# Four row blocks of w2 per quantization step, and attention heads divided straight from PSUM

## The reference

```
x = x + attn_a(layernorm(x))        # RWKV-like time mix, 16 heads
x = x + ffn(layernorm(x))           # BitNet-like, 1024 -> 4096 -> 1024
x = x + attn_b(layernorm(x))        # linear attention, 16 heads, chunks of 128
x = x + ffn(layernorm(x))           # the same FFN and weights again
```

```
scale = 1.0 / clip(mean(abs(w)), 1e-5)
wq = clip(round(w * scale), -1, 1) / scale
```

```
out = (inter_num + intra_num) / (inter_den + intra_den + 1e-6)
```

## Time and profile before

| | us |
|---|---|
| median of 3 runs (7890.95 to 7900.04) | 7897.22 |
| profiled execution, its own time | 7890.33 |
| span of its slowest core (core 4) | 7889.3 |
| spans of the other cores | 7857.3 to 7881.8 |
| quantization of w1, both passes (32.9 to 380.95) | 348.1 |
| quantization of w2, both passes (380.95 to 877.16) | 496.2 |
| attention a to the end | the rest |

### The profile page before, as it was taken

The page is one execution under the profiler, slowest core; times in us unless marked ns, Lnnn a source line. Parts: engine busy times, 40 slices in busy tenths (PEclk is TensorE's granted clock), DMA queues, the critical chain, the costliest instruction groups (busy, mean ns, idle before and its releaser), DMA issues.

```text
span 7889.3 us, 43212 instructions; the slowest of 8 cores (7857.3 to 7889.3 us)
## 1 busy us (share of the span) xinstructions
PE 2812.7 (36%) x12246; PEld 1203.9 (15%) x12420; DVE 2521.9 (32%) x5263; ACT 1027.8 (13%) x1504; POOL 154.0 (2%) x276
## 2 busy tenths in 40 slices
PE   0000045554234334443423444444414334433333
PEld 0000022222111111111101222222201111111111
DVE  3423343232522332223214333333342332223221
ACT  0101111110200111101102111111110111101110
POOL 0000000000000000000000000000000000000000
PEclk9999976666566666665655656566656656666666
DMA  4222300001011101110130000000011101110012
GB/s 156 106 94 80 120 0 1 1 1 45 0 43 43 34 13 39 43 43 12 31 127 1 1 1 1 1 1 1 1 44 43 31 13 42 43 43 15 28 43 83
DMA packets 92856, 288.49 MB, mean 37 GB/s; under 512 B 13244, under 2 KB 13772, under 8 KB 87506
## 3 DMA queue, kind: packets, MB, share of 16 engines
q1 hardware_dynamic: 67798, 201.83, 7.6%
q0 software_dynamic: 24832, 83.90, 3.6%
HBM read 260.48 MB, written 25.17 MB: 36 GB/s over the span
## 4 chain that ended last, share of the span: by engine, by line
DVE 30%; PE 29%; DMA 16%; issue 11%; ACT 11%; DVEq 1%; SPq 1%; ACTq 0%; POOLq 0%
DMA wbuf<-w2q_hbm 9%; PE pb L849 7%; PE pb L968 5%; DMA sA<-w_t 5%; PE pb L483 3%; PE pb L1206 2%; DVE arenaB L924 2%; ACT sA L866 2%; PE pbf L931 2%; ACT sB L912 2%; DVE arenaB L466 1%; PE pb L656 1%; DVEq L105 1%; ACT arenaB L1083 1%; DVE arenaB L935 1%
## 5 line engine op out<-in xcount | busy, mean ns | idle before, releaser
L968 PE MATMUL pb<-wbuf,arenaB 128*128 128x512 bf16 x2000 | 773.2, 544 | 556.2 <-DMA wbuf<-w2q_hbm 523.2
L849 PE MATMUL pb<-warena,arenaB 128*128 128x512 bf16 x1986 | 584.2, 461 | 196.2 <-ACT sA L866 132.1
L931 PE MATMUL pbf<-ident,arenaB 128*128 128x128 bf16 x1024 | 129.5, 306 | 1259.8 <-DVE arenaB L924 1188.0
L990 DVE TENSOR_TENSOR res<-res,pb 128x512 f32<-128x512 f32 x64 | 39.7, 683 | 1345.4 <-PE pb L980 1345.4
L968 PEld LDWEIGHTS pb<-wbuf,arenaB 128*128 128x128 bf16 x2048 | 223.8, 121 | 1097.4 <-issue 1050.3
L873 DVE TENSOR_REDUCE fcol<-sA 128x1 f32<-128x2048 f32 x32 | 73.1, 2286 | 887.1 <-ACT sA L866 887.1
L849 PEld LDWEIGHTS pb<-warena,arenaB 128*128 128x128 bf16 x2048 | 229.8, 114 | 543.4 <-issue 398.6
L931 PEld LDWEIGHTS pbf<-ident,arenaB 128*128 128x128 bf16 x1024 | 99.0, 137 | 1297.5 <-issue 1297.5
L483 PE MATMUL pb<-warena,arenaB 128*128 128x512 bf16 x752 | 211.1, 448 | 160.8 <-DVE arenaB L466 160.0
L958 POOL DMA_DIRECT2D wbuf<-w2q_hbm x256 | 137.7, 538 | 6668.0 <-PE pb L968 6217.5
L836 PE MATMUL pbf<-ident,arenaB 128*128 128x128 bf16 x256 | 32.4, 307 | 612.9 <-DVE arenaB L830 612.9
(11 more groups left out here) (219 smaller groups left out, 4490.3 us busy)
## 6 DMA issues: line engine op xcount, KB each, us to landing
wbuf<-w2q_hbm POOLq DMA_DIRECT2D x256, 256.0 KB, 2.9
wbuf<-w2q_hbm SPq DMA_DIRECT2D x256, 256.0 KB, 2.8
sA<-w_t SPq DMA_DIRECT2D x16, 2048.0 KB
sA<-w_t SPq DMA_DIRECT2D x64, 512.0 KB
warena<-w1q_hbm SPq DMA_DIRECT2D x2, 8192.0 KB
res<-x SPq DMA_DIRECT2D x1, 8192.0 KB
w1q_hbm<-arenaB SPq DMA_DIRECT2D x8, 1024.0 KB, 4.8
w2q_hbm<-arenaB SPq DMA_DIRECT2D x32, 256.0 KB, 2.1
```

What stands on the lines that cost most here:

```text
L849: mms.append((lambda e, ic=ic, ot=ot, o0=o0: e.matmul(p["pb%d" % ot][:], g["xqT"][:, 128 * ic:128 * ic + 128], W[:, 4096 * ic + o0:4096 * ...
L931: self.emit("tensor", lambda e, r=r, i=i: e.transpose(p["pbf"][:, 128 * i:128 * i + 128], g["hqb"][:, 1024 * r + 128 * i:1024 * r + 128 * ...
L968: mms.append((lambda e, hc=hc, bk=bk, oh=oh, buf=buf, hqT=hqT: e.matmul(p[bk][:], hqT[:, 128 * hc:128 * hc + 128], buf[:, 512 * oh:512 * o ...
```

## The change

There are two edits.

First, `wquant_one` takes a `batch` argument: one chunk becomes `batch` blocks of 128 rows, seen as `[128, batch, ncols]`. For w1 nothing changes (batch 1, 8 chunks). For w2 the call goes from 32 chunks of 128 x 1024 to 8 chunks of 128 x 4 x 1024, so each load brings 2 MB, each sum runs over 4096 columns, the rounding runs on two pieces of 2048 columns instead of four of 1024, and each store writes 1 MB.

Second, `attn_b_head_post` no longer copies `nd` to SBUF. The add of 1e-6 and the multiply read PSUM. The marks `ndf` and `ndb`, which let TensorE write into the bank again, move from the copy to the multiply, three operations later.

```
-    def wquant_one(self, dram_in, dram_out, ncols, nch, iswcol):
+    def wquant_one(self, dram_in, dram_out, ncols, nch, iswcol, batch=1):
...
-        src = self.dram[dram_in].rearrange("(a p) o -> p a o", p=128)
-        dst = self.dram[dram_out].rearrange("(a p) o -> p a o", p=128)
-        stage = g["sA"][:, 0:ncols]
-        nh = (ncols + 2047) // 2048
+        src = self.dram[dram_in].rearrange("(a q p) o -> p a q o", p=128, q=batch)
+        dst = self.dram[dram_out].rearrange("(a q p) o -> p a q o", p=128, q=batch)
+        ncols_eff = ncols * batch
+        stage = g["sA"][:, 0:ncols_eff]
+        st3 = stage.rearrange("p (q o) -> p q o", o=ncols)
+        nh = (ncols_eff + 2047) // 2048
         for a in range(nch):
-            self.emit("sync", lambda e, a=a: e.dma_start(out=stage, in_=src[:, a, :]),
+            self.emit("sync", lambda e, a=a, st3=st3: e.dma_start(out=st3, in_=src[:, a]),
                       wait=(("ve", self.now("ve")),), inc="dW", n=16)
...
-                w = min(2048, ncols - 2048 * hh)
+                w = min(2048, ncols_eff - 2048 * hh)
...
-            self.emit("sync", lambda e, a=a: e.dma_start(out=dst[:, a, :], in_=g["wq_bf"][:, 0:ncols]),
-                      wait=(("ve", self.now("ve")),), inc="dWs", n=16)
+            self.emit("sync", lambda e, a=a: e.dma_start(
+                out=dst[:, a], in_=g["wq_bf"][:, 0:ncols_eff].rearrange(
+                    "p (q o) -> p q o", o=ncols)),
+                wait=(("ve", self.now("ve")),), inc="dWs", n=16)
...
-        self.wquant_one("w2_t", "w2q_hbm", C, 32, g["fcol"][:, 41:42])
+        self.wquant_one("w2_t", "w2q_hbm", C, 8, g["fcol"][:, 41:42], batch=4)
...
         dc, rc = 42 + (h % 2), 44 + (h % 2)
-        nsl = g["sB"][:, 1024 + 128 * (h % 2):1024 + 128 * (h % 2) + 65]
-        self.emit("vector", lambda e, nd=nd, nsl=nsl: e.tensor_copy(out=nsl, in_=nd),
-                  wait=(ndtn,), inc="ve")
+        self.emit("vector", lambda e, nd=nd, dc=dc: e.tensor_scalar_add(
+            out=g["fcol"][:, dc:dc + 1], in0=nd[:, 64:65], scalar1=1e-6), wait=(ndtn,), inc="ve")
+        self.vchain([
+            lambda e, dc=dc, rc=rc: e.reciprocal(out=g["fcol"][:, rc:rc + 1],
+                                                 in_=g["fcol"][:, dc:dc + 1]),
+            lambda e, h=h, nd=nd, rc=rc: e.tensor_scalar_mul(
+                out=g["ob_b"][:, 64 * h:64 * h + 64], in0=nd[:, 0:64],
+                scalar1=g["fcol"][:, rc:rc + 1]),
+        ], wait0=(("ve", self.now("ve")),))
         self.hz["ndf%d" % (h % 8)] = ("ve", self.now("ve"))
         self.hz["ndb%d" % (h % 2)] = ("ve", self.now("ve"))
-        self.vchain([
...
```

More of the change, by code:

```diff
@@ L699, in wquant_one @@
         self.set_free("pb6", "sc")
-        nel = float(nch * 128 * ncols)
+        nel = float(nch * 128 * ncols_eff)
         self.vchain([
```

## The result

The changed kernel takes 7656.67 us (median of 8 runs, 7649.04 to 7672.79) against 7895.98 us (8 runs): a ratio of 0.9698, 95% interval 0.9687 to 0.9709, 239 us less. The prediction was 7679 us, within 7650 to 7727. Its sign and mechanism hold; it is 22 us too high. The saving of 239 us lies just beyond the 238 us that its bounds add up to, and inside the range only by the margin that it left for the measurement.

What follows compares the result with a forecast made beforehand. No engine was taken as the bound; an edit is worth what it takes out of a serial loop. Quantization 141 plus attention b 77 is 218 us off 7890.3, giving 7672, or 7679 with the median's 6.9; range 7650 to 7727.

Steps and rivals of the forecast that it cites:

- What bounds the kernel: Whole kernel: chain spread over all engines, none the bound; an edit is worth what it takes out of a serial loop.
- Pass 1: First pass of w2's quantization: 8 turns of 13.2 us, saving 61 us, bounds 55 to 66.
- step from 512 KB to 1 MB: w2's pass 1 loads: 3.99 to 5.54 us, so 1.55 us per 512 KB more, 8.6 us for 2 MB.
- Pass 2: Second pass of w2's quantization: 245 us against 325.5, saving 80 us, bounds 68 to 88.
- The price of short runs beside the store: w2's pass 2: 0.6 us more per load for 4 KB rows, 0.4 us for the store in 2 KB rows.
- Heads: Attention b: 0.30 us net saved per head over 256 heads in series, 77 us, bounds 51 to 84.
- The three terms: Each head of attention b: copy-to-add step of 0.33 us gone, add from PSUM no dearer, multiply 0.03 us more.
- The added wait: Attention b: line 1120's matmul now waits for the multiply; the pair takes until 0.82 us, line 1150 starts at 0.96.
- cover: Attention b: slack before the two delayed matmuls hold up line 1150, shrinking from about 1 us to 0.14 us.
- Dear PSUM reads: Attention b rival: PSUM reads dear or PE late, head gains 0.20 us or less; 7712 us at 0.17; 10%.
- Loads that are no better per byte: w2 quantization rival: a 2 MB load takes four times a small one, 16 us; 7795 us; 4%.
- The clock: PE stretches rival: less idle beforehand and denser heads lower the granted clock; at 0.54 some 7990 us; 2%.

Runs made afterwards that it cites:

- e12: Changed kernel with w2's chunks dealt so each partition takes four neighbouring rows, 16 KB per run on load; 7637.97 us, ratio 0.9698.
- e5: Kernel before, copy kept, with the marks `ndf` and `ndb` moved behind the multiply; 7880.96 us, ratio 0.9999.
- e6: Changed kernel with the mark moved further, behind the next head's mask; 7655.19 us, ratio 0.9715.
- e7: Changed kernel with the mark moved behind the next head's cast; 7710.98 us, ratio 0.9783.
- e8: Changed kernel with mask and cast fused into one operation that writes bf16 straight from PSUM; 7584.41 us, ratio 0.9625.
- e2: Kernel before with only the second edit: no copy, add and multiply read PSUM; 7800.92 us, ratio 0.9892.
- the prefetch version: Changed kernel with both quantizations rebuilt: 1 MB pieces, two staging and two store tiles, loads issued ahead; 7434.44 us, ratio 0.9439.

## Why the prediction was right

**What bounds the kernel.** Right. Both edits took what their serial loops held and nothing came back elsewhere: no untouched stage moved by more than 3 us but the first, which lost 5.7 us with code that did not change. The other runs with the same code for w1 gave 371 to 376 us, so that is spread between executions. It may be some 6 of the 22 us by which the forecast was high; passes 1 and 2 of w2 are 12 more.

**Pass 1.** The structure (turn = load + 4.6 us) was right to 0.1 us. The mis-sized term is the load, 8.6 us forecast and 7.6 measured, which is 8 us on the changed side. Its step from 512 KB to 1 MB was read from single loads that happened to be long. The 1 MB load of 5.54 us was issued behind two small DMAs, but this is not the reason: the same load behind the same two DMAs took 4.95 us on core 2 of the same trace (first row), and 5.0 us in the median over the eight cores of all fourteen profiles (4.7 to 7.0). A 1 MB load with no DMA ahead of it took 4.88 us on core 4 (second row) and 5.0 in the median:

```profile
894.69 4.95 DMA sC<-wk_t
...
4064.94 4.88 DMA sC<-wq_t
```

The lower end of the forecast load, w1's 7.94 us, was no fixed point either: with the same code w1's loads were shorter in the changed kernel's execution (7.5 us in the median over the cores, 8.1 in the kernel before; 7.5 to 8.1 over the runs), for instance on core 2:

```profile
105.06 7.55 DMA sA<-w_t
```

So the measured saving of 67.5 us lies outside the prediction's bounds for this pass, 55 to 66. The old side varies too: runs with the same pass 1 as before gave 160 to 168 us, with which the saving would be 59 to 67 us, around the forecast 61.

**Pass 2.** 80 against 85.6 us. First turn 28.9 forecast and 28.0 measured, later ones 30.9 and 30.6. The price of short runs beside the store was about right (0.7 to 0.8 us per turn in e12 against 1.0). Here too the old side varies, 323 to 330 us over the runs with the old pass 2. By the fit of the Trainium skill ("DMA: Bandwidth & Descriptors", section "Anatomy of one DMA"), 2.0 us and the bytes at 436 GB/s, made for loads that GpSimd issues, 2 MB would take 6.8 us and 512 KB 3.2 us, an estimate by that page. The traces have 7.6 to 7.7 and 3.5 to 3.8 us in the median, so for SP's loads here it is low by 0.3 to 0.9 us.

**Heads.** 77 forecast, 76.9 measured. The three terms each came out: the copy's step of 0.33 us gone, the add unchanged at 0.15, the multiply's step 0.03 to 0.04 longer. By the Trainium skill ("VectorE: DVE Perf Modes", sections "The TRN2 errata" and "Why PSUM operands drop a tier") it would have been 0.17 us per head, the prediction's estimate by that page. Its fixed part, 120 cycles against 58, is not there: the add of one column took 150 ns from PSUM and 154 from SBUF. Its other part fits: 64 columns of f32 from PSUM at one per cycle would cost 33 ns more, an estimate by that page of the Trainium skill, and the multiply went from 255 to 284 ns.

**The added wait.** Right that it costs nothing (e5), wrong in how thin its cover is. The cover was put at 0.14 us and is about 0.28 (e6, e7), because the end of a matmul's bar is not when its queue is free. The error did no harm here. With one more DVE step removed (e8) the right number decides whether 36 or 66 us are gained.

**The rivals.** Dear PSUM reads: out (e2). Loads that are no better per byte: out, 2 MB take 7.6 us, not 16. The clock: TensorE's granted clock stays at its mix of the two levels (1.2 and 2.4 GHz) where it has work, for instance in FFN 1 of the changed kernel. It is 0.62 there, as it is in the same stage of the kernel before (2150 to 3950 us) and in the earlier trace rows:

```profile
2000.00:3800.00 1800.00, 704.52 (x2459) 265.10 (x2508) 520.29 (x792) 228.31 (x240) 60.20 (x112) 0.62 0.11 33
```

The price of this rival was added up wrong: at a clock of 0.54, 2290 x (0.62 / 0.54 - 1) is 339 us, which gives 8018 us and not 7990.

## What to carry to other kernels

When two stages do the same work in different numbers of turns, the faster one is a measured model of the other; take its turn and correct only what differs. In a chain of small operations each removed step is worth its start-to-start distance, not its busy time, until another engine's queue is in the way; find that point from the distance between starts on that engine. And read the price of a transfer from its median over cores: the same 1 MB load was 4.95 us on one core and 5.54 on another.

## What the runs showed that I had not expected

- A matmul shown as 0.21 to 0.27 us long lets the next start 0.12 to 0.13 us after its own start in most heads, with 65 columns as with 128. This is at the lower of the two clock levels (1.2 GHz), as the windows of the changed kernel show for the first eight turns of the head loop above:

```profile
4184.72:4201.30 16.58, 5.86 (x32) 3.33 (x32) 9.29 (x48) 0.00 (x0) 0.00 (x0) 0.50 0.01 1
```

The Trainium skill ("TensorE: Matmul & The Clock Gate", section "Wait — 56ns, not 53.3ns?") gives 106.7 ns from start to start for 128 columns at that level. The traces have 125 ns, with a weight load between the two, so the measurement is 18 ns longer. Had the prediction used the page's figure in place of the bar's end, its cover would have come to 0.32 us, an estimate by that page and much nearer to 0.28 than the 0.14 was.
- Loads from HBM by SP, alone in flight, medians over the cores in different runs: 3.5 to 3.8 us for 512 KB, 4.9 for 1 MB, 7.6 to 7.7 for 2 MB in rows of 4 KB. In rows of 16 KB 2 MB took 7.6 us for w2 (e12) and 7.5 to 8.1 for w1, so the length of the rows makes less of a difference than one execution does to the next.
- The mean granted clock over the span fell from 0.667 to 0.661 and to 0.652 in the prefetch version, although the stages with matmuls kept their own (0.61 to 0.63 in windows of attention a and of both FFN stages, in all three kernels). The mean over the span holds the idle quantization at 1.00, so it falls when that stage gets shorter, and says nothing on how the matmuls ran.
